# Where VectorE takes the B rows of a state-space scan from: PSUM by TensorE, or SBUF by a broadcasting DMA

## What is computed

```python
dbl = jnp.einsum('ble,fe->blf', xc, x_proj)
dt, Bm, Cm = jnp.split(dbl, [DT_RANK, DT_RANK + D_STATE], axis=-1)
delta = jax.nn.softplus(jnp.einsum('blr,er->ble', dt, dt_w) + dt_b)
def step(h, inp):
    xt, dt_, bt, ct = inp
    dA = jnp.exp(dt_[..., None] * A)
    h = dA * h + dt_[..., None] * bt[:, None, :] * xt[..., None]
    y = jnp.einsum('bdn,bn->bd', h, ct)
    return (h, y)
```

## Time and profile before

| | |
|---|---|
| median of 3 runs | 3478.18 us (3476.75 to 3483.45) |
| the profiled execution: own time, span | 3478.78 us, 3477.0 us |
| VectorE (DVE) busy | 3042.4 us, 88% |
| ScalarE (ACT) busy | 3106.2 us, 89% |
| GpSimd (POOL) busy | 2824.1 us, 81% |
| TensorE (PE) matmul busy | 2952.8 us, 85% |
| DMA queue of the kernel | 25.4% of the 16 engines |

### The profile page before, as it was taken

How to read it: one execution, slowest core, us unless ns; L and a number is a source line. 1 busy time by engine, 2 the same in 40 slices (tenths; PEclk the granted TensorE clock), 3 DMA queues, 4 the chain that set the end, 5 groups by cost and what they waited for, 6 DMA issues and landing times.

```text
span 3477.0 us, 53162 instructions
## 1 busy us (share of the span) xinstructions
PE 2952.8 (85%) x18432; PEld 2224.8 (64%) x18432; DVE 3042.4 (88%) x2456; ACT 3106.2 (89%) x5825; POOL 2824.1 (81%) x1701
## 2 busy tenths in 40 slices
PE   5888888888888888888888888888888888888885
PEld 3666666666666666666666666666666666666664
DVE  3889889889889888898898898899898988888986
ACT  4989999999989999999999998999999999999984
POOL 2788888888888888788788888888887888888886
PEclk9999999999999999999999999999999999999998
DMA  2222222222222222222222222222222222222221
GB/s 72 89 72 92 86 86 85 81 83 91 86 86 85 78 91 86 81 88 83 82 86 86 86 91 73 91 85 86 87 89 74 91 86 85 85 81 83 87 81 48
DMA packets 102319, 290.59 MB, mean 84 GB/s; under 512 B 11387, under 2 KB 36262, under 8 KB 102054
## 3 DMA queue, kind: packets, MB, share of 16 engines
q1 hardware_dynamic: 102054, 287.19, 25.4%
HBM read 276.91 MB, written 10.24 MB: 83 GB/s over the span
## 4 chain that ended last, share of the span: by engine, by line
ACT 33%; PE 31%; DVE 20%; issue 14%; POOL 1%; DVEq 0%; SPq 0%; DMA 0%; ACTq 0%; POOLq 0%
ACT da L697 13%; DVE hc L941 10%; PE g_ps L329 8%; DVE g_ps L928 8%; ACT w L643 7%; PE y_ps L329 5%; ACT L684 5%; PE m_ps L362 3%; PE m_ps L413 3%; PE m_ps L371 3%; PE m_ps L329 3%; PE m_ps L429 2%; PE m_ps L391 2%; DVE stats L914 2%; ACT s L667 1%
## 5 line engine op out<-in xcount | busy, mean ns | idle before, releaser
L834 POOL TENSOR_TENSOR hc<-hc,c_all 128x1000 f32<-128x1000 f32 x1024 | 2350.3, 2313 | 522.3 <-DVE hc L941 508.4
L941 DVE TENSOR_TENSOR_SCAN hc<-da,g_ps 128x1012 f32<-128x1012 f32 x1024 | 2274.6, 2253 | 91.4 <-ACT da L697 18.9
L697 ACT ACTIVATE da<-delta,a_neg 128x498 f32<-128x498 f32 x2048 | 1332.9, 700 | 9.0 <-DVE hc L941 7.3
L329 PEld LDWEIGHTS y_ps<-ident,hc 128*125 128x125 f32 x8192 | 1027.7, 190 | 238.8 <-issue 164.3
L329 PE MATMUL y_ps<-ident,hc 128*125 128x128 f32 x8192 | 1081.7, 275 | 2.2 <-POOL hc L834 2.2
L643 ACT ACTIVATE w<-ut,bt 125x256 f32<-125x256 f32 x2048 | 892.8, 497 | 2.9 <-ACT ut L630 0.4
L329 PE MATMUL g_ps<-ident,w 125*128 125x125 f32 x4096 | 547.3, 277 | 370.7 <-DVE hc L941 280.5
L329 PEld LDWEIGHTS g_ps<-ident,w 125*128 125x128 f32 x4096 | 443.9, 142 | 427.1 <-DVE hc L941 326.1
L928 DVE TENSOR_TENSOR g_ps<-u,g_ps 128x1000 f32<-128x1000 f32 x512 | 608.2, 1188 | 80.6 <-PE g_ps L455 80.3
L362 PE MATMUL m_ps<-zt,convw 128*128 128x500 f32 x1024 | 475.6, 587 | 0.7 <-ACT zt L573 0.7
L362 PEld LDWEIGHTS m_ps<-zt,convw 128*128 128x128 f32 x1024 | 190.5, 191 | 148.7 <-issue 121.9
(11 more groups left out here) (62 smaller groups left out, 2314.5 us busy)
## 6 DMA issues: line engine op xcount, KB each, us to landing
c_all<-c_rows SPq DMA_DIRECT2D x512, 500.0 KB, 3.6
xin<-x_t SPq DMA_DIRECT2D x32, 375.0 KB, 3.5
out<-out_sb SPq DMA_DIRECT2D x32, 250.0 KB
c_rows<-dbl SPq DMA_DIRECT2D x64, 31.2 KB, 1.6
c_all<-f_conv_w SPq DMA_DIRECT2D x1, 512.0 KB
c_all<-b_conv_w SPq DMA_DIRECT2D x1, 512.0 KB
hc<-f_in_w SPq DMA_DIRECT2D x1, 128.0 KB
inw<-f_in_w SPq DMA_DIRECT2D x1, 128.0 KB
```

What stands on the lines that cost most here:

```text
L329: return pe.matmul(dst, src, ident[0:rows, 0:rows], start=first, stop=last, is_transpose=True, skip_group_check=True)
L697: op = act.activation(states(da[n % RING])[j].rearrange("p (s t) -> p s t", s=SC)[:, :, 1:T], steps, ACT.Exp, scale=a_neg[:, p % 2, db, 2 ...
L834: pool.tensor_tensor(hc, hc, c_all[:, pair % CRING], ALU.mult).then_inc(hc_ready, 1)
L941: dve.tensor_tensor_scan(h[n % HRING][:, 0:UC], da[n % RING][:], g_ps[n % 2][:, 0:UC], 0.0, ALU.mult, ALU.add).then_inc(scanned, 1)
```

## The change

The selecting matmuls, the three bfloat16 parts and their copies and subtractions go. SyncE writes B and C together to DRAM, and spreads the B rows of pairs 0, 1, 3 and 5 over 128 partitions into two new SBUF buffers `b_all`. `times_b` reads u and `b_all`, both in SBUF, and writes the product to `g_ps`. The jobs of a phase are put at other units, and `all_jobs` is sorted by these units. `W_POOL` stays empty, so `make_w` on POOL, which is rewritten, issues nothing.

```diff
-CONV, GATES, XPROJ, BT, SPLIT1, Y0, SPLIT2, Y1, DT, U0, U1, UT0, UT1 = 0, 4, 5, 6, 6, 6, 7, 8, 9, 11, 12, 13, 14
-TURN, TAIL0, TAIL1, TOKENS = 10, 11, 14, 15
-STATS_Z, POW_Z, NORM_Z = 1, 3, 8
-ADD_Z, STATS_Q, POW_Q, NORM_Q = 0, 1, 3, 5
-RESIDUAL, STATS_OUT, POW_OUT, NORM_OUT, STORE = 6, 8, 9, 11, 12
+CONV, GATES, XPROJ, DT, SOFTPLUS, BT, Y0, Y1, U0, U1, UT0, UT1, GATED0, GATED1 = 0, 4, 5, 6, 7, 6, 8, 9, 9, 10, 12, 13, 10, 11
+YT = (2, 3)
+TURN, TAIL0, TAIL1, TOKENS = (0, 13), (0, 15), (1, 4), (1, 15)
+STATS_Z, POW_Z, NORM_Z = (0, 1), (0, 3), (0, 8)
+ADD_Z, STATS_Q, POW_Q, NORM_Q = (1, 6), (1, 7), (1, 8), (1, 9)
+RESIDUAL, STATS_OUT, POW_OUT, NORM_OUT, STORE = (1, 10), (1, 12), (1, 13), (1, 15), (1, 15)
...
+STRAIGHT = [r for r in range(PAIRS) if r not in TURNED]
...
+def spread_b_step(q):
+    m, v = divmod(q, len(STRAIGHT))
+    free = 0
+    if q >= BRING:
+        before, u = divmod(q - BRING, len(STRAIGHT))
+        free = UNITS * before + 2 * STRAIGHT[u] + 2
+    return max(UNITS * (m - 1) + XPROJ + 2, free)
...
-        parts = [sb(f"parts{j}", [K2, TC], BF16) for j in range(2)]
+        b_all = sb("b_all", [128, BRING, 2, TC])
...
-                sp.dma_start(c_rows[m % 2], dbl[NS:2 * NS, :]).then_inc(c_written, 16)
+                    sp.wait_ge(dbx_ready, straight(UNITS * (m - 1) - 1))
                     sp.wait_ge(hc_ready, UNITS * (m - 1))
+                sp.dma_start(bc_rows[m % 2], dbl[0:2 * NS, :]).then_inc(bc_written, 16)
...
+            def spread_b(q):
+                m, v = divmod(q, len(STRAIGHT))
+                r = STRAIGHT[v]
+                sp.wait_ge(bc_written, 16 * (m + 1))
+                if q >= BRING:
+                    sp.wait_ge(dbx_ready, 2 * (q - BRING) + 2)
+                rows = bc_rows[m % 2][2 * r:2 * r + 2, :]
+                sp.dma_start(b_all[:, q % BRING], rows.partition_broadcast(128)).then_inc(b_ready[q % BRING], 16)
...
-                    pe.matmul(g[:, 0:TC], pick[:, 2 * r, :], parts[p % 2][:], start=True, stop=True)
-                    pe.matmul(g[:, BANK:UC], pick[:, 2 * r + 1, :], parts[p % 2][:],
-                              start=True, stop=True).then_inc(b_filled, 1)
...
-                act.activation(parts[p % 2][:], m[0:K2, 0:TC],
-                               ACT.Copy).then_inc(drained[bank_of("xproj", p, 0)], 1)
...
-                dve.wait_ge(b_filled, n + 1)
-                g = paired(g_ps[n % 2])
-                dve.tensor_tensor(g, u[p % 2][:, db, :].unsqueeze(1).broadcast_to([128, 2, TC]), g,
-                                  ALU.mult).then_inc(dbx_ready, 1)
+                dve.wait_ge(b_ready[q // 2 % BRING], 16 * (q // 2 // BRING + 1))
+                if n > 1:
+                    dve.wait_ge(scanned, n - 1)
+                dve.tensor_tensor(paired(g_ps[n % 2]), u[p % 2][:, db, :].unsqueeze(1).broadcast_to([128, 2, TC]),
+                                  b_all[:, q // 2 % BRING], ALU.mult).then_inc(dbx_ready, 1)
...
-                    if m > 0 and k in (Y0 + 1, Y1 + 1):
-                        gated(m - 1, 0 if k == Y0 + 1 else 1)
+                    if m > 0 and k in (GATED0, GATED1):
+                        gated(m - 1, 0 if k == GATED0 else 1)
```

More of the change, by code:

```diff
@@ L86, in w_count, with straight @@
     return m * len(table) + sorted(table).index(r) + 1
-def b_products(n):
+STRAIGHT = [r for r in range(PAIRS) if r not in TURNED]
+def straight(n):
     m, k = divmod(n, UNITS)
-    here = [j for j in range(k + 1) if j // 2 not in TURNED]
-    return m * 2 * (PAIRS - len(TURNED)) + len(here)
+    return m * 2 * len(STRAIGHT) + len([j for j in range(k + 1) if j // 2 in STRAIGHT])
+def spread_b_step(q):
[5 more added lines that the diff above has]
+    return max(UNITS * (m - 1) + XPROJ + 2, free)
@@ L211, in audio_tower_kernel @@
         x_loaded = sem("x_loaded")
-        c_written = sem("c_written")
+        bc_written = sem("bc_written")
+        b_ready = [sem(f"b_ready{j}") for j in range(BRING)]
         c_ready = [sem(f"c_ready{j}") for j in range(CRING)]
@@ L491, in _ @@
                 i, d = divmod(m, 2)
-                front, more = m + 1 < PHASES, d == 0 and i + 1 < NCH
+                front = m + 1 < PHASES
                 for k in range(UNITS):
@@ L529, in _ @@
                             turn_u(m + 1, 1)
[L530 removed]
+                    if i + 1 < NCH and (d, k) == TURN:
+                        turn(i + 1)
+                    if i > 0 and (d, k) == TAIL0:
+                        out_proj(i - 1, 0)
+                    if i > 0 and (d, k) == TAIL1:
                         out_proj(i - 1, 1)
[L532 removed]
+                    if i + 2 < NCH and (d, k) == TOKENS:
                         tokens(i + 2)
@@ L970, in _ @@
                     scan(n)
-                    if more and k == STATS_Z:
+                    if i + 1 < NCH and (d, k) == STATS_Z:
                         wait_drained(dve, "tokens", i + 1, 0)
```

193 lines of the change are left out of this document (82 added, 111 removed).

## The result

The changed kernel takes **3494.02 us** (median of 7 runs, 3488.99 to 3498.07) where the kernel before took 3478.29 in the same session (7 runs, 3476.36 to 3483.45): a ratio of **1.0044, 95% interval 1.0033 to 1.0056**, slower by 0.44%. The forecast was 3593 us. The direction holds and the time lies in the range, but the loss is 16 us where 115 were forecast.

What follows compares the result with a forecast made beforehand. Four engines in a ring bound the kernel, none full; with exclusion POOL would set the pace. Sum: 3478.8 + 35.4 (POOL overflow) + 77 (hand-overs) + 2 (start) = 3593 us, range 3260 to 3680.

Steps and rivals of the forecast that it cites:

- The likeliest case, exclusion: A two-SBUF-operand VectorE product and a POOL instruction exclude each other: 3593 us, 3516 to 3670, chance 0.50.
- POOL's 2.13 ns per column: POOL's two-operand SBUF products, twice VectorE's 1.04 with one operand there, taken as evidence that a second operand has a price.
- POOL's busy time plus the products' over 97%: Share of the 64-phase stretch, given as one sign that the exclusion forecast is right.
- With exclusion POOL takes over the pace, and the gains of VectorE and ACT turn into waits: Phase stretch: products' 608.2 us in POOL's 572.8 idle overflow by 35.4 us; 512 hand-overs add 77.
- The hand-over: Between VectorE's product and POOL: 0.15 us for each of 512 products, 77 us in all.
- The partial case: VectorE and POOL exclude each other only while columns stream: 3453 us, 3398 to 3508, chance 0.12.
- No exclusion: VectorE and POOL read SBUF undisturbed, ACT sets the stretch: 3276 us, 3231 to 3356, chance 0.22.
- TensorE's term: Selecting matmuls and subtractions go, 436 us; TensorE busy about 2478 us, 2726 at clock 0.90; worth nothing by itself.
- POOL first: POOL keeps its turn while work is queued, each run's first product waits: 432 us more, 4025 us, chance 0.13.
- Late rows: DMA spreads of B rows land too late for the products: at most 256 us on 3276, about 3530, chance 0.03.
- The 2 us of the start: Before the phases, the first product needs the first spread of B rows: loss between 0 and 3.1, taken as +2 us.
- `gated`'s 205 us: VectorE's 205.2 us of waits for `y_back` on TensorE nearly all go when `gated` moves from one unit behind to two.

Runs made afterwards that it cites:

- e9: Changed kernel's DMA path for B, with the old order of jobs, chunk end and ACT's shares put back: 3753.8 us, ratio 1.0789 to the kernel before.
- e10: Changed kernel's path for B in the old order, with the product's second operand in PSUM (B left out): 3370.82 us, ratio 0.9695 to the kernel before.
- e1: Changed kernel with the product's second operand taken from PSUM instead of SBUF (B left out): 3344.62 us, ratio 0.9615 to the kernel before.
- e8: Changed kernel with VectorE's product over only 500 of 1000 columns (the other half left out): 3390.25 us, ratio 0.9743 to the kernel before.
- e5: Changed kernel sending only the first two of 256 spreads of B rows, later products rereading those buffers: 3503.82 us, ratio 1.007 to the kernel before.
- e3: Kernel before with only the two gating products moved one unit later on VectorE: 3573.76 us, ratio 1.027 to the kernel before.
- e12: Changed kernel with only the chunk end (output projection, norms, residual, store) put back as early as before: 3745.57 us, ratio 1.0773 to the kernel before.
- e14: Changed kernel with POOL's power job of the first norm moved from unit 3 to 5: 3513.39 us, ratio 1.01 to the kernel before.
- e15: Changed kernel with POOL's power job of the first norm moved from unit 3 to 8, its norm to 10: 3493.54 us, ratio 1.0046 to the kernel before.

## Why the prediction was right in direction and wrong in size

- **The likeliest case, exclusion, is the right one.** Its signs are there: the product at 1687 ns, the C product at 2676, POOL's wait down from 508.4 to 136.8 (under 100 was forecast). The Trainium skill (SBUF — State Buffer, section "Who interferes with whom") says that the later of the two blocks; the two places of the timeline agree, with 1.18 us for a product that came first and 2.13 for one that came second, but for the 0.11 to 0.15 us that the second one saves. One ground of the prediction was none: POOL's 2.13 ns per column says nothing of VectorE's second operand, since a VectorE product with two SBUF operands that comes first takes 1.18 us, as the one with one SBUF operand did. And the sign "POOL's busy time plus the products' over 97%" told nothing, since it held before the change (3416.1 of 3380.7).
- **The step that failed: "With exclusion POOL takes over the pace, and the gains of VectorE and ACT turn into waits".** Its terms were 35.4 and 77 us, and they charged all of the exclusion, 608.2 + 77 = 685 us, to POOL. The loss fell on both engines instead: 428.1 on POOL and 255.7 on VectorE. That the two make 683.8 together does not confirm the term: in e9 the same products cost the two engines 749 us more busy time than in e10. POOL comes to 2807.9 + 428.1 = 3236.0, 157 us under the stretch and not 35.4 over it, so the two terms had no such place in the sum. VectorE is the fuller of the two, 96% of the stretch against POOL's 95%, and neither is full. Both are on the chain of work that ended last, VectorE with 28% and POOL with 10%, where they had 20% and 1% before. The prediction had VectorE's number, 3131 us without the waits for `gated` and the fill, and did not use it in this case: 3131 + 256 = 3387, against 3392.9 measured, and with the 100.3 us outside the stretch within 7 us of the time. That it comes so near is partly luck. Without exclusion VectorE does not come down to 3131 us, because 117 us of other waits come up (e1); these pass only while a product is held up.
- **Why POOL bears less.** The prediction made POOL give up each product in full. The two places of the timeline show how it is shared: a product that comes second loses on VectorE's account (0.95 us), one that comes first costs POOL 0.81 of its 1.18.
- **The hand-over** of 0.15 us does not exist as a loss: e8 and the two places of the timeline show 0.11 to 0.15 us less than the rest of the other's instruction, in place of 0.15 more. (The 115 ns that the prediction takes from the Trainium skill, SBUF — State Buffer, stand there in the section "A bandwidth-pool intuition that's wrong (but worth ruling out)", for a DMA that a VectorE instruction holds up and not for two instructions.) The partial case was right that part of the time is free for the other and that POOL is not full, and its 3453 is nearer than 3593, but by luck: its price of VectorE's waits (222 us, 255.7 measured) was put on three products a phase, where half of all products take over 1545 ns.
- **No exclusion**, 3276 with 3231 to 3356, is excluded by the durations, and its range was sound: e1 gives 3344.6. The time stays near the upper end, with VectorE waiting 139.7 us for TensorE's transposes, which no term of the prediction had.
- **TensorE's term was wrong.** Forecast was 2478 us in the stretch, or 2726 at the lower clock; measured were 2836. Two things are on record. The granted clock was 0.92 where it had been 0.99, and the matmuls are longer: those of `y_ps` 291 ns in the mean, before 275. And the 436 us were taken off in full, though the groups of TensorE overlap: before, they add up to 3461 us where the engine is busy for 2953. What this cost in time is not shown; VectorE's waits for transposes are small here (23.3 us).
- **POOL first** (4025 us) is excluded: the longest product is 3.19 us, under 1.18 + 2.31, so a waiting product gets the next turn. **Late rows** are excluded by the waits, VectorE's one wait for `b_all` being the start, and by e5.
- **The 2 us of the start** came out as a number only (100.3 us outside the stretch against 98.1). The start became 1.2 us shorter (61.1 against 62.3), the first spread leaving at 56.68 and not at 61.84; the end became 3.4 us longer (37.4 against 34.0).

```profile
56.68 0.38 SPq L318 DMA_DIRECT2D b_all<-bc_rows  x1
```

- **`gated`'s 205 us**: gone, as forecast, but a wait that goes is not time won. The move alone loses about 95 us (e3), and in e12 `gated` waits 7.7 us in all, but VectorE waits 257.3 us in front of its scans.

**What stays open.** Why the same exclusion holds up the products for 256 us in the new order and 381 in the old, and why the old order's waits absorb none of it, is described but not settled. In every run with the exclusion and a piece of the old order POOL still waits 416 to 545 us for scans, in the changed kernel 137: there POOL is mostly behind and seldom idle. Whether that is the cause was not tried apart; e14 and e15 show only that moving POOL's power job out of unit 3 does not help.
